# Five of sixteen feed-forward jobs turned in 32x32 blocks on VectorE and through DRAM, with layer norms and low parts moved in the order

## The chip, the cores and the metric

The kernel runs on one core of one Trainium2 chip. The time is the device time of one execution in microseconds (us). Engines are named as in the profile: PE is TensorE's matmuls and PEld its weight loads, DVE is VectorE, ACT is ScalarE, POOL is GpSimd, and SP is the queue from which most transfers are issued.

## The reference, cut to what matters

x is 8 batches of 512 tokens by 128 features, float32. Three layers follow one another; each adds to x.

```
x = x + 0.5 * spikes(relu(LN(x) @ W_fc.T)**2 @ W_proj.T)     # feed-forward, "first"
x = x + attention(LN(x))                                     # per batch, see below
x = x + 0.5 * spikes(relu(LN(x) @ W_fc.T)**2 @ W_proj.T)     # feed-forward, "second"

attention(h): h = LN(h)*gamma + beta; keys = h@Wk.T + bk; values = h@Wv.T + bv
    w = exp((keys@Wka.T + bka)/sqrt(128)); w = w / cumsum(w, tokens)
    return cumsum(w * keys, tokens) * values
```

The spike count of a value is a staircase with five levels, made from two straight lines and a maximum.

## The kernel before, in words

**Jobs.** One feed-forward layer of one batch is a job. There are 16: jobs 0 to 7 are the first layer of batches 0 to 7, jobs 8 to 15 the second. Job j works in lane j mod 2, and a lane has one set of buffers. Attention b is the attention of batch b.

**A job.** Layer norm's statistics are made on DVE (L559 to L572), the inverse deviation and the normalised tokens on POOL (L380, L386). TensorE then turns the four 128x128 tiles of `normed` into the bank `work` (`ff_turn`, L866), because a product needs the features on the partitions. ACT rounds the turned input to its high part `in_hi` (L451) and DVE subtracts it for the low part `in_lo` (L632). TensorE expands to four chunks of `hidden`, each as three products of high and low parts (L853, L854, L857); ACT makes the relu (L455) and its square (L460) of each chunk; TensorE contracts the squares into `work`, in four chunks of 8 instructions (L932), of which chunk 3 ends the job's y. ACT makes the two stairs from it (L464, L467), DVE the maximum, the count and the new x.

**The order.** Nothing is scheduled at run time. Every engine has a loop over steps -3 to 18, and its instructions are written out in that order; semaphores alone tie the engines together. In step i TensorE does, in this order: turn job i; contract chunk 2 of job i-1; turn attention b of the step into `att_work` (L963); contract chunk 3 of job i-1; expand chunks 0 and 1 of job i; turn back the attention of step i-2 (L987); the key attention (a product of three); expand chunks 2 and 3; contract chunk 0; the keys (three); contract chunk 1; the values of the attention of step i-1 (three). `ATT_STEP` gives the steps of attentions 0 to 7: 3, 4, 5, 7, 8, 9, 10, 11.

ACT in step i: the square `share_bank` for the attention of step i-1 (L516, waits for `pooled` of the attention before it), the stairs of job i-1, the relus and squares of job i with the attention's weight and guess between them, then `in_hi` of job i+1 and the attention's high part.

DVE in step i: layer norm of job i+1; `weight_key` of the attention of step i-1 (L706); `pooled` of step i-2 (L723); `in_lo` of job i; `attended` (L731); `att_lo` (L637); `near_share` (L713); the new x of job i-2 (L693); statistics of the next attention with `highest` between (L672); adding the attention to x (L736); `share_key` (L718); `count` (L685); the scan `weight_sum` (L699); in steps 0 to 2 also the attention's weights and biases.

POOL in step i: normalises job i+2, then the attention of step i+2, then makes `guess_sum` and `guess_share` of the attention of step i+1 (L408, L416).

**Waits that matter here.** TensorE turns attention b into `att_work` only when `weight_key` of attention b-1 has read that bank (L960). The transfer that brings x is issued on SP for all batches at the start; the results are stored from SP as they come.

Of the kernel before, what the change touches and what calls it, by code (L numbers as in the profile page):

```python
# [24 lines left out]
P = 128  # L25
F32 = mybir.dt.float32
# [12 lines left out]
FF_JOBS = [("first", b) for b in range(8)] + [("second", b) for b in range(8)]  # L39
ATT_STEP = [3, 4, 5, 7, 8, 9, 10, 11]  # L40
CONTRACT_ORDER = (0, 1, 2, 3)

DVE_SQUARES = [(), ()]
NEXT_TO_LAST_DVE_SQUARES = (1,)
# [6 lines left out]
class FeedForward:  # L51


    def __init__(self, i):
        self.layer, self.batch = FF_JOBS[i]
        self.index, self.lane, self.turn = i, i % 2, i // 2
        self.dve_squares = DVE_SQUARES[i in ATT_STEP] if i < len(FF_JOBS) - 2 else NEXT_TO_LAST_DVE_SQUARES
        self.pool_squares = [c for c in POOL_SQUARES[i in ATT_STEP] if c not in self.dve_squares]
        self.act_squares = [c for c in CONTRACT_ORDER if c not in self.dve_squares and c not in self.pool_squares]
        self.is_last = i == len(FF_JOBS) - 1  # L60
        if self.is_last:
            self.pool_squares, self.dve_squares, self.act_squares = (LAST_SQUARES[e] for e in ("pool", "dve", "act"))

# [4 lines left out]

def feed_forward(i):
    return [FeedForward(i)] if 0 <= i < len(FF_JOBS) else []  # L70


def attention(i):
# [87 lines left out]
def macaron_kernel(nc, x, wk, bk, wka, bka, wv, bv, gamma, beta, w_fc, w_proj, out):  # L161
# [26 lines left out]
    with ExitStack() as ctx:  # L188
        def sb(name, shape, dtype=F32):
            return ctx.enter_context(nc.sbuf_tensor(name, shape, dtype))  # L190
# [50 lines left out]
        rstd = {k: sb(f"rstd_{k}", [P, NT]) for k in KINDS}  # L241
        normed = {k: sb(f"normed_{k}", [P, NT, P]) for k in KINDS}

        in_hi = [sb(f"in_hi{l}", [P, S], F32R) for l in LANES]
        in_lo = [sb(f"in_lo{l}", [P, S], F32R) for l in LANES]
        relu = [sb(f"relu{l}", [P, NC, S]) for l in LANES]
# [41 lines left out]
        ln_args_made, rstd_made = sems("ln_args_made", KINDS), sems("rstd_made", KINDS)  # L288
        normed_made = sems("normed_made", KINDS)
        turned, hi_made, lo_made = sems("turned", KINDS), sems("hi_made", KINDS), sems("lo_made", KINDS)  # L290
        hidden_made, relu_made = sems("hidden_made", LANES), sems("relu_made", LANES)
        squares_act, squares_pool = sems("squares_act", LANES), sems("squares_pool", LANES)
        squares_dve = sems("squares_dve", LANES)
# [17 lines left out]
        def wait_relu(engine, j, c):  # L311

            engine.wait_ge(relu_made[j.lane], NC * j.turn + c + 1)

        def bank_of_hidden(j, c):
            return hidden[(NC * j.index + c) % HIDDEN_BANKS]
# [23 lines left out]
        @block.sync  # L340
        def _(sp):
            load_first_half(sp, 0)
            load_fc_half(sp, 0)
            load_proj_half(sp, 0)
            sp.dma_start(x_of["first"][1][:], x_tiles[1]).then_inc(x_loaded[1], 16)
            for k, w in enumerate((wk, wv, wka)):
                sp.dma_start(att_raw[:, k, :], w).then_inc(att_loaded, 16)
            sp.dma_start(x_of["first"][2][:], x_tiles[2]).then_inc(x_loaded[2], 16)
            for k, v in enumerate((bk, bv, bka, gamma, beta)):
                sp.dma_start(vectors[:, k:k + 1], v.rearrange("(p a) -> p a", a=1)).then_inc(vectors_loaded, 16)  # L350
            for b in range(3, NB):
                sp.dma_start(x_of["first"][b][:], x_tiles[b]).then_inc(x_loaded[b], 16)
            for b in range(NB - 1):
                sp.wait_ge(x_made["out"], b + 1)
                sp.dma_start(out_tiles[b], x_of["out"][b][:]).then_inc(out_stored, 16)
            for t in range(NT):
                sp.wait_ge(x_tile_made, t + 1)
                sp.dma_start(out_tiles[NB - 1][:, t, :], x_of["out"][NB - 1][:, t, :]).then_inc(out_stored, 16)
            sp.wait_ge(out_stored, 16 * (NB - 1 + NT))
# [3 lines left out]
        def _(pool):  # L363
# [14 lines left out]
            def normalise(kind, turn, source):  # L378
# [4 lines left out]
                if turn:  # L383
                    pool.wait_ge(turned[kind], turn)
                for t in range(NT):
                    nc.gpsimd.tensor_scalar(normed[kind][:, t, :], source[:, t, :], neg_mean[kind][:, t:t + 1],  # L386
                                            rstd[kind][:, t:t + 1], ALU.add, ALU.mult).then_inc(normed_made[kind], 1)

            def ff_normalise(j):
                if j.index == 0:  # L390
                    first_inverse_deviation(j)
                else:
                    normalise(j.lane, j.turn, x_of[j.layer][j.batch])

            def att_normalise(b):
                normalise("att", b, x_of["att"][b])

            def ff_squares(j):
                for c in j.pool_squares:
# [17 lines left out]
                                        ALU.mult).then_inc(guess_share_made, 1)  # L417

            for i in range(FIRST_STEP, STEPS):
                for j in feed_forward(i + 2):  # L420
                    ff_normalise(j)
                for b in attention(i + 2):
                    att_normalise(b)
                for b in attention(i + 1):
                    att_guess_sum(b)
                    att_guess_share(b)
                for j in feed_forward(i):
                    ff_squares(j)
# [3 lines left out]
        def _(act):  # L432
# [13 lines left out]
            def ff_hi(j):  # L446
                if j.index == 0:
                    first_hi(j)
                    return
                act.wait_ge(turned[j.lane], j.turn + 1)  # L450
# [105 lines left out]
        def _(dve):  # L556
# [67 lines left out]
            def ff_lo(j):  # L624
                if j.index == 0:
                    dve.wait_ge(hi_made[j.lane], 1)
                    nc.vector.tensor_tensor(in_lo[j.lane][:, HALF:S], first_second_half[:, HALF:S],
                                            in_hi[j.lane][:, HALF:S].bitcast(F32),
                                            ALU.subtract).then_inc(lo_made[j.lane], 1)
                    return  # L630
                dve.wait_ge(hi_made[j.lane], j.turn + 1)
                nc.vector.tensor_tensor(in_lo[j.lane][:], work[j.lane][:], in_hi[j.lane][:].bitcast(F32),  # L632
                                        ALU.subtract).then_inc(lo_made[j.lane], 1)

            def att_part_lo(b):
                dve.wait_ge(hi_made["att"], b + 1)
# [147 lines left out]
            for i in range(FIRST_STEP, STEPS):  # L784
# [3 lines left out]
                for j in feed_forward(i + 1):  # L788
                    if j.index == 0:
                        first_layer_norm(j, 0)  # L790
                        fc_split_ident()
                        first_layer_norm(j, 1)
                        first_normalise(j, 0)
                        first_fc_low_part()
                        first_normalise(j, 1)
                        first_half_lo(j)
                        other_fc_low_parts()
                    else:
                        ff_layer_stats(j)
                for j in feed_forward(i + 1):  # L800
                    if j.index > 0:
                        ff_layer_args(j)
                for b in attention(i - 1):
                    att_weight_key(b)
                for b in attention(i - 2):
                    att_pool(b)
                for j in feed_forward(i):
                    if j.index > 0:
                        ff_lo(j)
                for b in attention(i - 2):  # L810
                    att_product(b)
                for b in attention(i):
# [37 lines left out]
        def _(pe):  # L850
# [6 lines left out]
                return nc.tensor.matmul(dst, w_hi, x_lo, start=False, stop=True)  # L857

            def ff_turn(j):

                if j.turn:
                    pe.wait_ge(stairs_made[j.lane], STAIRS_A_JOB * j.turn)
                for t in range(NT):
                    pe.wait_ge(normed_made[j.lane], NT * j.turn + t + 1)
                    bank_of = first_second_half if j.index == 0 and t >= HALF_TILES else work[j.lane]
                    last = nc.tensor.transpose(bank_of[:, t * P:(t + 1) * P], normed[j.lane][:, t, :], ident[:])  # L866
                    if j.index == 0 and t == HALF_TILES - 1:
                        last.then_inc(first_turned, 1)
                        turn_proj(range(0, NC // 2))
                last.then_inc(turned[j.lane], 1)  # L870
# [203 lines left out]
```

## Time and profile before

| | us |
|---|---|
| median of 3 executions | 147.83 |
| lowest, highest | 147.3, 364.3 |
| the profiled execution | 147.76 |
| its span, first to last instruction | 146.0 |

| engine | busy us | share of the span |
|---|---|---|
| PE | 140.3 | 96% |
| PEld | 126.1 | 86% |
| DVE | 117.3 | 80% |
| ACT | 113.8 | 78% |
| POOL | 95.8 | 66% |

The granted clock of TensorE was 0.999 of full speed over the span. Matmuls overlap one another, so their durations add up to more than the time they take: what one of them costs in a row of matmuls is the distance between two starts. The same holds, more weakly, for DVE and ACT. The DMA engines were busy in the first tenth of the span and with the stores of the end.

### The profile page before, as it was taken

The numbers are of one execution on the slowest core, as the hardware profiler recorded it, in microseconds if no ns is written. First come the engines' busy times: TensorE is split into PE (matmuls) and PEld (weight loads), VectorE is DVE, ScalarE is ACT, GpSimd is POOL, SyncE is SP. The second block draws the span as 40 slices with busy tenths as digits, with TensorE's granted clock in tenths as the row PEclk, the third lists the DMA queues.
The fourth block names the chain that finished last, engine by engine and source line by source line (L and its number), as shares of the span: only waits on it lengthen the run. The fifth ranks groups of instructions, "written<-read, shape, count | busy, mean of one in ns | idle before, by whom it ended". The sixth has DMA issues, their size and how long they took to land.

```text
span 146.0 us, 2901 instructions
## 1 busy us (share of the span) xinstructions
PE 140.3 (96%) x945; PEld 126.1 (86%) x945; DVE 117.3 (80%) x403; ACT 113.8 (78%) x215; POOL 95.8 (66%) x141
## 2 busy tenths in 40 slices
PE   7899999999999999999999999999999999999990
PEld 7689898989989899998988989889789898979790
DVE  3894559388699989999779999999999978453674
ACT  3278877789896996959979697796796977977761
POOL 1439247929999929894998989989967952520300
PEclk9999999999999999999999999999999999999999
DMA  4975000000000000000000000020020102020222
GB/s 140 270 203 161 4 2 0 0 0 4 2 0 2 0 4 2 0 0 0 4 0 0 0 0 7 0 72 0 2 76 0 57 15 72 7 72 0 72 72 72
DMA packets 10510, 5.09 MB, mean 35 GB/s; under 512 B 1152, under 2 KB 10496, under 8 KB 10496
## 3 DMA queue, kind: packets, MB, share of 16 engines
q1 hardware_dynamic: 9808, 4.53, 10.7%
q10 hardware_dynamic: 688, 0.39, 0.9%
q8 instruction: 7, 0.11, 0.3%
q14 instruction: 7, 0.06, 0.1%
HBM read 2.82 MB, written 2.10 MB: 34 GB/s over the span
## 4 chain that ended last, share of the span: by engine, by line
PE 48%; DVE 25%; issue 14%; POOL 6%; DMA 3%; POOLq 1%; ACT 1%; ACTq 1%; DVEq 0%
PE work L932 19%; PE hidden L853 5%; PE hidden L857 5%; PE hidden L854 5%; POOL normed L386 4%; DMA proj_raw<-in_L_ffn_W_proj_dram 3%; DVE weight_sum L699 3%; PE work L866 2%; POOL rstd L380 2%; DVE stats L559 2%; DVE pooled L723 2%; DVE share_bank L713 2%; DVE weight_key L706 2%; DVE share_bank L718 2%; DVE stats_att L559 2%
## 5 line engine op out<-in xcount | busy, mean ns | idle before, releaser
L932 PE MATMUL work<-proj_t,square 128*128 128x128 f32 x480 | 61.2, 275 | 0.0
L932 PEld LDWEIGHTS work<-proj_t,square 128*128 128x128 f32 x480 | 58.8, 192 | 2.4 <-ACT square L460 0.4
L460 ACT ACTIVATE square<-relu 128x512 f32<-128x512 f32 x60 | 37.7, 641 | 0.7
L455 ACT ACTIVATE relu<-hidden 128x512 f32<-128x512 f32 x64 | 36.7, 606 | 0.1
L853 PE MATMUL hidden<-in_hi,fc_lo 128*128 128x512 f32 (+1 forms) x66 | 27.5, 417 | 0.1
L857 PE MATMUL hidden<-in_lo,fc_hi 128*128 128x512 f32 (+1 forms) x66 | 25.6, 387 | 0.0
L854 PE MATMUL hidden<-in_hi,fc_hi 128*128 128x512 f32 (+1 forms) x66 | 25.4, 385 | 0.0
L380 POOL TENSOR_TENSOR rstd<-var_eps,minus_half 128x4 f32<-128x4 f32 x15 | 15.2, 1012 | 14.7 <-DVE neg_mean L572 14.7
L632 DVE TENSOR_TENSOR in_lo<-work,in_hi 128x512 fp32r<-128x512 f32 x15 | 10.2, 680 | 12.3 <-ACT in_hi L451 12.3
L386 POOL TENSOR_SCALAR normed_att<-x_att,neg_mean_att,rstd_att 128x128 f32<-128x128 f32 x32 | 18.1, 578 | 0.8
L386 POOL TENSOR_SCALAR normed<-x_second,neg_mean,rstd 128x128 f32<-128x128 f32 x32 | 16.9, 540 | 0.8
L464 ACT ACTIVATE stairs<-work 128x512 int16<-128x512 f32 (+1 forms) x16 | 9.2, 574 | 7.9 <-PE work L932 6.8
L386 POOL TENSOR_SCALAR normed<-x_first,neg_mean,rstd 128x128 f32<-128x128 f32 x28 | 14.7, 536 | 0.7
L857 PEld LDWEIGHTS hidden<-in_lo,fc_hi 128*128 128x128 f32 x66 | 12.4, 188 | 2.9
L853 PEld LDWEIGHTS hidden<-in_hi,fc_lo 128*128 128x128 f32 x66 | 12.5, 189 | 2.0 <-issue 0.3
L854 PEld LDWEIGHTS hidden<-in_hi,fc_hi 128*128 128x128 f32 x66 | 12.5, 189 | 1.7
L408 POOL TENSOR_TENSOR guess_sum<-weight_sum,guess 128x512 f32<-128x512 f32 x8 | 10.2, 1276 | 5.1 <-ACT guess L509 5.0
L380 POOL TENSOR_TENSOR rstd_att<-var_eps_att,minus_half 128x4 f32<-128x4 f32 x8 | 8.1, 1007 | 8.0 <-DVE neg_mean_att L572 8.0
L451 ACT ACTIVATE in_hi<-work 128x512 fp32r<-128x512 f32 x15 | 8.9, 592 | 4.9 <-PE work L866 4.9
L416 POOL TENSOR_TENSOR guess_share<-weight_key,guess 128x512 f32<-128x512 f32 x8 | 10.2, 1272 | 0.1
L699 DVE TENSOR_TENSOR_SCAN weight_sum<-ones,weight 128x512 f32<-128x512 f32 x8 | 9.7, 1217 | 0.4 <-ACT weight L499 0.4
L723 DVE TENSOR_TENSOR_SCAN pooled<-ones,share_bank 128x512 f32<-128x512 f32 x8 | 9.7, 1210 | 0.0
(118 smaller groups left out, 245.8 us busy)
## 6 DMA issues: line engine op xcount, KB each, us to landing
x_first<-_attn_hidden_states_dram SPq DMA_DIRECT2D x7, 256.0 KB, 4.0
out_dram<-x_out SPq DMA_DIRECT2D x7, 256.0 KB, 2.2
out_dram<-x_out SPq DMA_DIRECT2D x4, 64.0 KB, 1.5
x_first<-_attn_hidden_states_dram ACTq DMA_DIRECT2D x1, 128.0 KB, 2.7
x_first<-_attn_hidden_states_dram SPq DMA_DIRECT2D x1, 128.0 KB, 2.4
fc_raw<-in_L_ffn_W_fc_dram SPq DMA_DIRECT2D x1, 128.0 KB, 2.8
fc_raw<-in_L_ffn_W_fc_dram ACTq DMA_DIRECT2D x1, 128.0 KB, 3.3
proj_raw<-in_L_ffn_W_proj_dram SPq DMA_DIRECT2D x1, 128.0 KB, 3.1
```

The costliest lines, as they stand in the source:

```text
L380: nc.gpsimd.tensor_tensor(rstd[kind][:], var_eps[kind][:], minus_half[:], ALU.pow).then_inc(rstd_made[kind], 1)
L386: nc.gpsimd.tensor_scalar(normed[kind][:, t, :], source[:, t, :], neg_mean[kind][:, t:t + 1], rstd[kind][:, t:t + 1], ALU.add, ALU.mult).t ...
L408: nc.gpsimd.tensor_tensor(guess_sum[b % 2][:], weight_sum[b % ATT_SETS][:], guess[b % 2][:], ALU.mult).then_inc(guess_sum_made, 1)
L416: nc.gpsimd.tensor_tensor(guess_share[b % 2][:], weight_key[b % 2][:], guess[b % 2][:], ALU.mult).then_inc(guess_share_made, 1)
L455: nc.scalar.activation(relu[j.lane][:, c, :], bank_of_hidden(j, c)[:], ACT.Relu).then_inc(relu_made[j.lane], 1)
L460: nc.scalar.activation(square[j.lane][:, c, :], relu[j.lane][:, c, :], ACT.Square).then_inc(squares_act[j.lane], 1)
L699: nc.vector.tensor_tensor_scan(weight_sum[b % ATT_SETS][:], ones[:], weight[b % ATT_SETS][:], 0.0, ALU.mult, ALU.add).then_inc(sum_made, 1)
L723: nc.vector.tensor_tensor_scan(pooled[:], ones[:], share_bank[:], 0.0, ALU.mult, ALU.subtract).then_inc(pooled_made, 1)
L853: nc.tensor.matmul(dst, w_lo, x_hi, start=True, stop=False)
L854: nc.tensor.matmul(dst, w_hi, x_hi, start=False, stop=False)
L857: return nc.tensor.matmul(dst, w_hi, x_lo, start=False, stop=True)
L932: last = nc.tensor.matmul(work[j.lane][:, tokens], square[j.lane][:, c, tokens], proj_t[:, c, :], start=(c == 0 and t == 0), stop=(c == NC ...
```

## The change

Jobs 3 to 7 (`BLOCK_TURNED`) are not turned by TensorE any more. For each of them DVE transposes the 32x32 blocks of `normed` (`ff_block_turn`); SP stores the result to DRAM and loads it back in four transfers, one for each 32 partitions, with the blocks in their places (rows of 512 bytes); ACT and DVE then make `in_hi` and `in_lo` from that buffer in SBUF, in a permuted order, instead of from the bank `work`.

With it the order on DVE and POOL changes. `LAYER_NORM_STEP` and `LAYER_NORM_PLACE` set the layer norm of jobs 3 to 7 to: job 3 step 1, middle; job 4 step 1, end; job 5 step 2, middle; job 6 step 2, end; job 7 step 5, top (before: steps 2 to 6, at the top). All other jobs keep theirs. The block turns stand at the end of steps 1, 2, 2, 3 and 5, ahead of the scan `weight_sum`. `in_lo` of jobs 3 to 7 moves to the very top of the job's step, ahead of the layer norm, `weight_key` and `pooled`. The place of `in_hi` on ACT, the end of step j-1, stays.

```diff
+LAYER_NORM_STEP = [-1, 0, 1, 1, 1, 2, 2, 5, 7, 8, 9, 10, 11, 12, 13, 14]
+LAYER_NORM_PLACE = ['top', 'top', 'top', 'middle', 'end', 'middle', 'end', 'top', 'top', 'top', 'top', 'top', 'top', 'top', 'top', 'top']
+BLOCK_TURN_STEP = [1, 2, 2, 3, 5]
+BLOCK_TURNED = [3, 4, 5, 6, 7]
+QUARTER = 32
+BLOCK_SETS = 3
...
+        def turned_before(j):
+            return j.before(lambda other: not other.by_blocks)
+        def blocks_before(j):
+            return j.before(lambda other: other.by_blocks)
+        def by_token(tile):
+            return tile[:].rearrange("p (a t j) -> p t a j", a=P // QUARTER, t=NT)
+        def in_quarters(tile):
+            return tile[:].rearrange("p (t a j) -> p t a j", a=P // QUARTER, t=NT)
...
(SP, ahead of the stores of the results)
+            for k, index in enumerate(BLOCK_TURNED):
+                j = FeedForward(index)
+                sp.wait_ge(blocks_made[j.lane], blocks_before(j) + 1)
+                sp.dma_start(block_rows[k].ap(), blocks[k % BLOCK_SETS][:]).then_inc(blocks_stored[k], 16)
+                sp.wait_ge(blocks_stored[k], 16)
+                quarters = block_rows[k].ap().rearrange("(a i) (b n) -> b i a n", i=QUARTER, b=P // QUARTER)
+                if k >= BLOCK_SETS:
+                    last = FeedForward(BLOCK_TURNED[k - BLOCK_SETS])
+                    sp.wait_ge(lo_made[last.lane], last.turn + 1)
+                for q in range(P // QUARTER):
+                    part = block_turned[k % BLOCK_SETS][q * QUARTER:(q + 1) * QUARTER, :]
+                    sp.dma_start(part.rearrange("p (a n) -> p a n", n=P),
+                                 quarters[q]).then_inc(blocks_loaded[k], 16)
...
(POOL)
+            def wait_ff_read(j):
+                for last in feed_forward(j.index - 2):
+                    if last.by_blocks:
+                        pool.wait_ge(blocks_made[j.lane], blocks_before(j))
+                    else:
+                        pool.wait_ge(turned[j.lane], turned_before(j))
...
             for i in range(FIRST_STEP, STEPS):
-                for j in feed_forward(i + 2):
+                for j in layer_norms(i + 1, "top", "middle"):
                     ff_normalise(j)
                 for b in attention(i + 2):
                     att_normalise(b)
+                for j in layer_norms(i + 1, "end"):
+                    ff_normalise(j)
...
(ACT, ff_hi)
+                if j.by_blocks:
+                    k = BLOCK_TURNED.index(j.index)
+                    act.wait_ge(blocks_loaded[k], 16 * (P // QUARTER))
+                    act.wait_ge(hidden_made[j.lane], NC * j.turn)
+                    nc.scalar.activation(in_quarters(in_hi[j.lane]), by_token(block_turned[k % BLOCK_SETS]),
+                                         ACT.Copy).then_inc(hi_made[j.lane], 1)
+                    return
...
(DVE, ff_lo and the turn)
+                if j.by_blocks:
+                    nc.vector.tensor_tensor(in_quarters(in_lo[j.lane]), by_token(block_turned[BLOCK_TURNED.index(j.index) % BLOCK_SETS]),
+                                            in_quarters(in_hi[j.lane]).bitcast(F32),
+                                            ALU.subtract).then_inc(lo_made[j.lane], 1)
+                    return
+            def ff_block_turn(j):
+                if j.by_blocks:
+                    dve.wait_ge(normed_made[j.lane], NT * (j.turn + 1))
+                    k = BLOCK_TURNED.index(j.index)
+                    if k >= BLOCK_SETS:
+                        dve.wait_ge(blocks_stored[k - BLOCK_SETS], 16)
+                    rows = blocks[k % BLOCK_SETS]
+                    nc.vector.transpose(rows[:].rearrange("p (b t j) -> p t b j", b=P // QUARTER, t=NT),
+                                        normed[j.lane][:].rearrange("p t (b i) -> p t b i", i=QUARTER)
+                                        ).then_inc(blocks_made[j.lane], 1)
...
(DVE, the loop)
+                for j in feed_forward(i):
+                    if j.by_blocks:
+                        ff_lo(j)
+                for j in layer_norms(i, "top"):
+                    if j.index > 0:
                         ff_layer_stats(j)
-                for j in feed_forward(i + 1):
-                    if j.index > 0:
                         ff_layer_args(j)
                 for b in attention(i - 1):
                     att_weight_key(b)
                 for b in attention(i - 2):
                     att_pool(b)
                 for j in feed_forward(i):
-                    if j.index > 0:
+                    if j.index > 0 and not j.by_blocks:
                         ff_lo(j)
+                for j in layer_norms(i, "middle"):
+                    ff_layer_stats(j)
+                    ff_layer_args(j)
...
+                for j in layer_norms(i, "end"):
+                    ff_layer_stats(j)
+                    ff_layer_args(j)
+                for j in block_turns(i):
+                    ff_block_turn(j)
                 for b in attention(i):
                     att_sum(b)
...
(PE)
             def ff_turn(j):
+                if j.by_blocks:
+                    return
...
(PE, ff_contract)
+                if j.by_blocks and c == 0:
+                    pe.wait_ge(stairs_made[j.lane], STAIRS_A_JOB * j.turn)
```

## Rows read from the trace of the kernel before

**Rows 1.** The page: busy us (share of the span) xinstructions.
```profile
PE 140.3 (96%) x945; PEld 126.1 (86%) x945; DVE 117.3 (80%) x403; ACT 113.8 (78%) x215; POOL 95.8 (66%) x141
```
**Rows 2.** Timeline of PE, steps 3 to 5: start us, us, engine, line, what, count.
```profile
28.57 0.60 PE L963 MATMUL att_work<-ident,normed_att 128*128 128x128 f32 x4
...
35.82 0.60 PE L866 MATMUL work<-ident,normed 128*128 128x128 f32 x4
36.26 1.06 PE L932 MATMUL work<-proj_t,square 128*128 128x128 f32 x8
37.15 0.60 PE L963 MATMUL att_work<-ident,normed_att 128*128 128x128 f32 x4
...
45.11 0.60 PE L866 MATMUL work<-ident,normed 128*128 128x128 f32 x4
...
46.44 0.60 PE L963 MATMUL att_work<-ident,normed_att 128*128 128x128 f32 x4
```
**Rows 3.** Timeline of PE, step 11: the same columns, and idle time before it.
```profile
102.60 0.66 PE L963 MATMUL att_work<-ident,normed_att 128*128 128x128 f32 x4 [0.29 <-DVE weight_key L706]
```
**Rows 4.** Timeline of ACT, steps 3 to 6.
```profile
35.98 0.62 ACT L460 ACTIVATE square<-relu 128x512 f32<-128x512 f32 x1
36.50 0.58 ACT L451 ACTIVATE in_hi<-work 128x512 fp32r<-128x512 f32 x1
...
44.70 0.62 ACT L460 ACTIVATE square<-relu 128x512 f32<-128x512 f32 x1
...
56.58 0.69 ACT L516 ACTIVATE share_bank<-guess_sum,off_centre 128x512 f32<-128x512 f32 x1 [0.49 <-DVE pooled L723]
57.34 0.60 ACT L464 ACTIVATE stairs<-work 128x512 int16<-128x512 f32 x1
59.26 1.17 ACT L460 ACTIVATE square<-relu 128x512 f32<-128x512 f32 x2
...
62.10 0.63 ACT L460 ACTIVATE square<-relu 128x512 f32<-128x512 f32 x1
```
**Rows 5.** Timeline of DVE, steps 1, 2, 4 and 5.
```profile
14.10 0.69 DVE L632 TENSOR_TENSOR in_lo<-work,in_hi 128x512 fp32r<-128x512 f32 x1 [2.04 <-ACT in_hi L451]
...
22.10 0.71 DVE L693 SCALAR_TENSOR_TENSOR x_att<-count,x_first 128x512 f32<-128x512 uint16 x1
...
24.30 0.15 DVE L572 TENSOR_REDUCE neg_mean_att<-moments_att 128x4 f32<-128x4 f32 x1
...
28.56 0.69 DVE L632 TENSOR_TENSOR in_lo<-work,in_hi 128x512 fp32r<-128x512 f32 x1 [2.39 <-ACT in_hi L451]
...
43.78 0.85 DVE L559 BATCH_NORM_STATS2 stats<-x_first 128x6 f32<-128x128 f32 x4
...
45.16 0.74 DVE L706 SCALAR_TENSOR_TENSOR weight_key<-att_work,kv_bias,weight 128x512 f32<-128x512 f32 x1
45.82 1.21 DVE L723 TENSOR_TENSOR_SCAN pooled<-ones,share_bank 128x512 f32<-128x512 f32 x1
46.95 0.67 DVE L632 TENSOR_TENSOR in_lo<-work,in_hi 128x512 fp32r<-128x512 f32 x1
47.53 0.74 DVE L731 SCALAR_TENSOR_TENSOR attended<-att_value,kv_bias,pooled 128x512 f32<-128x512 f32 x1
```
**Rows 6.** Timeline of POOL: job 2, attention 0, and the square of step 15.
```profile
12.50 1.01 POOL L380 TENSOR_TENSOR rstd<-var_eps,minus_half 128x4 f32<-128x4 f32 x1
13.61 1.73 POOL L386 TENSOR_SCALAR normed<-x_first,neg_mean,rstd 128x128 f32<-128x128 f32 x4
...
137.39 1.11 POOL L401 TENSOR_TENSOR square<-relu 128x512 f32<-128x512 f32 x1 [8.91 <-ACT relu L455]
```
**Rows 7.** Line L644 on DVE: min/median/max ns, first and last start us.
```profile
L644 DVE TENSOR_TENSOR square<-relu x3: 680/693/1220, 130.8 to 139.0; 128x512 f32<-128x512 f32 x3
```
**Rows 8.** DMA issues: what, queue, count, KB each, us to landing.
```profile
x_first<-_attn_hidden_states_dram SPq DMA_DIRECT2D x7, 256.0 KB, 4.0
out_dram<-x_out SPq DMA_DIRECT2D x7, 256.0 KB, 2.2
```

More of the change, by code:

```diff
@@ L60, in __init__ @@
         self.is_last = i == len(FF_JOBS) - 1
+        self.by_blocks = i in BLOCK_TURNED
         if self.is_last:
@@ L70, in feed_forward, with layer_norms, block_turns @@
     return [FeedForward(i)] if 0 <= i < len(FF_JOBS) else []
+def layer_norms(i, *places):
+    return [FeedForward(k) for k in range(len(FF_JOBS))
+            if LAYER_NORM_STEP[k] == i and LAYER_NORM_PLACE[k] in places]
+def block_turns(i):
+    return [FeedForward(k) for k in BLOCK_TURNED if BLOCK_TURN_STEP[BLOCK_TURNED.index(k)] == i]
 def attention(i):
@@ L242, in macaron_kernel @@
         normed = {k: sb(f"normed_{k}", [P, NT, P]) for k in KINDS}
+        blocks = [sb(f"blocks{k}", [P, S]) for k in range(BLOCK_SETS)]
+        block_turned = [sb(f"block_turned{k}", [P, S]) for k in range(BLOCK_SETS)]
+        block_rows = [nc.dram_tensor(f"block_rows{k}", (P, S), F32) for k in range(len(BLOCK_TURNED))]
         in_hi = [sb(f"in_hi{l}", [P, S], F32R) for l in LANES]
@@ L290, in macaron_kernel @@
         turned, hi_made, lo_made = sems("turned", KINDS), sems("hi_made", KINDS), sems("lo_made", KINDS)
+        blocks_made = sems("blocks_made", LANES)
+        blocks_stored = [sem(f"blocks_stored{k}") for k in range(len(BLOCK_TURNED))]
+        blocks_loaded = [sem(f"blocks_loaded{k}") for k in range(len(BLOCK_TURNED))]
         hidden_made, relu_made = sems("hidden_made", LANES), sems("relu_made", LANES)
@@ L376, in first_inverse_deviation, with normalise @@
                                         minus_half[:, HALF_TILES:NT], ALU.pow).then_inc(rstd_made[j.lane], 1)
-            def normalise(kind, turn, source):
+            def normalise(kind, turn, source, wait_read):
                 pool.wait_ge(ln_args_made[kind], 2 * (turn + 1))
@@ L382, in normalise @@
                 pool.wait_ge(rstd_made[kind], turn + 1)
-                if turn:
-                    pool.wait_ge(turned[kind], turn)
+                wait_read()
                 for t in range(NT):
@@ L387, in normalise, with wait_att_read @@
                                             rstd[kind][:, t:t + 1], ALU.add, ALU.mult).then_inc(normed_made[kind], 1)
+            def wait_ff_read(j):
[4 more added lines that the diff above has]
+                        pool.wait_ge(turned[j.lane], turned_before(j))
+            def wait_att_read(b):
+                if b:
+                    pool.wait_ge(turned["att"], b)
             def ff_normalise(j):
@@ L392, in ff_normalise @@
                 else:
-                    normalise(j.lane, j.turn, x_of[j.layer][j.batch])
+                    normalise(j.lane, j.turn, x_of[j.layer][j.batch], lambda: wait_ff_read(j))
             def att_normalise(b):
-                normalise("att", b, x_of["att"][b])
+                normalise("att", b, x_of["att"][b], lambda: wait_att_read(b))
             def ff_squares(j):
@@ L449, in ff_hi @@
                     return
-                act.wait_ge(turned[j.lane], j.turn + 1)
+                if j.by_blocks:
[5 more added lines that the diff above has]
+                    return
+                act.wait_ge(turned[j.lane], turned_before(j) + 1)
                 nc.scalar.activation(in_hi[j.lane][:], work[j.lane][:], ACT.Copy).then_inc(hi_made[j.lane], 1)
@@ L797, in _ @@
                         other_fc_low_parts()
-                    else:
+                for j in feed_forward(i):
[3 more added lines that the diff above has]
+                    if j.index > 0:
                         ff_layer_stats(j)
-                for j in feed_forward(i + 1):
-                    if j.index > 0:
                         ff_layer_args(j)
```

## The prediction

> **What bounds the kernel now.** I read the page's busy shares first, then the timelines of PE, ACT, DVE and POOL side by side, then the DMA issues. PE is busy 96% of the span [rows 1], but a share alone does not say that it never waits. The timeline does: a turn takes 0.44 us of issue and a chunk of contraction 0.89 (35.82, 36.26, 37.15 [rows 2]). Three products of 512 columns take 0.69 (estimate: twelve products, the turn and 32 contractions of a job, with the attention's parts, fill the 9.29 us from 35.82 to 45.11: 0.44 + 4 x 0.89 + 0.44 + 7 x 0.69 = 9.27 [rows 2]). So step 4 has no gap on PE, and up to step 9 I find none. Later the only attention wait of note is for `weight_key`, 0.29 us at 102.60 [rows 3]. PE is the bound; the other engines' order matters exactly where PE asks for their results. Below, T is the start of the attention's turn on PE (28.57, 37.15, 46.44 in steps 3, 4, 5 [rows 2]), P the start of the step.
>
> **What is removed.** Five turns of 0.44: 2.2 us, all on the bound. Nothing else can be won but the small waits of the last steps, under 1 us together (0.29 is the largest I saw [rows 3]).
>
> **What is added, with cover.** Five block turns on DVE. The trace has none; from below the nearest is a 128x512 pass with PSUM input, 0.58 from start to start (46.95 to 47.53 [rows 5]), from above the scan, 45.82 to 46.95, 1.13. I take 0.6, since a turn is one pass as `in_lo` is. The first four end in steps 1 to 3, where DVE had 2.39 us of idle ahead of `in_lo` [rows 5]; they cost nothing, and each could cost its excess over 0.6 if that cover went. The round trip: a store of 256 KB lands after 2.2 us, a load after 4.0 [rows 8], 6.2 together, in four parts now. Job 3 is turned at about 19.6 (working below), loaded by 25.9, and ACT wants it at 28.0 (its `in_hi` of 0.58 had just ended when DVE's `in_lo` started at 28.56 [rows 5]): 2 us to spare. Job 7 is turned 6 us after T of step 5 and wanted 17 after it: 5 us to spare. SP has nothing else queued until the stores of the second layer. `in_hi` reads SBUF: 0.6 as before, bounds 0.5 and 0.7. `in_lo` has two SBUF inputs now; 0.58 to 0.9 (L644, the other such pass, has median 0.69 and once 1.22 [rows 7]). I take 0.58, as its median is that of `in_lo`.
>
> **What is moved, and what then waits.** This decides. `in_lo` of jobs 3 to 7 now stands ahead of `weight_key` on DVE, and waits for `in_hi`, which ACT makes as the last feed-forward work of the step before. DVE used to be ahead there: in step 4 it did the layer norm and `weight_key` and only then came to wait. Queued behind the wait are `weight_key`, `pooled` and `attended`; PE's attention turn waits for the first, ACT's `share_bank` for the second, PE's turn back for the third.
>
> *Step 3, POOL.* DVE was free for `x_att` at 22.10 and had `neg_mean_att` at 24.30 [rows 5]. Job 5's layer norm, 1.38 us (43.78 to 45.16 [rows 5]), now precedes both: 25.8. But POOL has job 5 first. It gets its statistics at 22.1 + 1.38 = 23.5; a normalisation takes 12.50 to 15.34, 2.84 [rows 6]; so attention 0 is ready at 23.5 + 2 x 2.84 = 29.2. PE starts that turn at 28.57 - 0.44 = 28.13 and would have its last tile at 28.5. Loss about 0.6 (bounds 0 and 1.2). Likewise job 3: after `in_lo` of job 1, 14.10 + 0.58 [rows 5], a layer norm of 1.38 and 2.84 on POOL make 18.9, and the turn ends at 19.6.
>
> *Step 4.* `in_hi` starts 0.52 after the last square (35.98, 36.50 [rows 4]), 7.93 after T of step 3, and ACT's chain from there on hangs on PE's contraction, so this distance stays. It ends at T + 8.53. Then `in_lo` 0.58, `weight_key` 0.75 (45.16 [rows 5]), signals 0.06 as at 102.60: PE can turn at T + 9.9. It would like to at 35.82 + 0.89 - 28.57 = 8.1. Loss 1.8.
>
> *Step 5.* The same, with the last square 7.55 after T (44.70 - 37.15 [rows 2, 4]): `in_hi` ends at T + 8.67, `in_lo` 9.27, and now job 7's layer norm, 1.38, also stands ahead of `weight_key`: 10.65 + 0.75 + 0.06 = 11.5. PE would like 45.11 + 0.89 - 37.15 = 8.85. Loss 2.6.
>
> *Step 6* has no attention turn. T of step 5 is zero here. PE reaches the step at 8.40. The block turn delays the scan and with it ACT by 0.15; `in_hi` ends at 8.8, `in_lo` 9.4, `weight_key` 10.1, `pooled` 11.3. `share_bank`, the stairs, the relus and the squares of ACT follow at the distances of rows 4 (56.58, 57.34, 59.26): square 0 starts at 14.1 and ends at 14.7. PE wants to contract at 13.4. Loss 1.3.
>
> *Step 7.* ACT comes from its stairs to `in_hi` in 5.28 (57.34 to 62.10, and 0.52 [rows 4]), so `in_hi` ends 0.8 after P. `in_lo` 0.6, job 8's layer norm 1.38, `pooled` 1.13, `attended` 0.74: P + 4.7, where the turn back wants it at 0.89 + 0.44 + 0.89 + 1.39 = 3.6; the low part behind it adds 0.15. Loss 1.3. In step 8 the scan of step 7 and the next layer norm leave DVE 0.3 late. After that job 8 is turned by PE again, DVE and PE meet at `att_lo`, and the old order holds: nothing more.
>
> **The sum.** 0.6 + 1.8 + 2.6 + 1.3 + 1.3 + 0.3 = 7.9, less 2.2: +5.7 on the profiled execution's 147.76, which is the median of 147.83 for practical purposes (the outlier of 364.3 left out). That is **153.5 us**.
>
> One term of it could be larger. In the trace a DVE pass with two SBUF inputs went to 1.22 us once [rows 7], beside POOL's 1.11 us square [rows 6]; the others took 0.69. `guess_sum` runs on POOL about when the new `in_lo` starts in steps 4 to 6, so up to 0.3 in each is open.
>
> The Trainium skill, "SBUF — State Buffer", section "Who interferes with whom", has it that a VectorE instruction with two SBUF inputs and a GpSimd instruction that reads SBUF exclude one another, the later one waiting for the earlier to end. By that rule `in_lo` is held each time, the loss is about 0.9 in all and the time 154.4; by the median of the row it is not held and stays at 153.5. The 1.22 us of the trace agrees with the rule.
>
> The skill's "VectorE: DVE Perf Modes", section "Rules for kernel authors", would leave a 128x128 transpose to TensorE where PSUM will do. No row of this case shows the two ways side by side.
>
> **Rivals.**
> - *The turns come off and nothing waits.* If `in_hi` were there whenever DVE gets to `in_lo`, `weight_key` would not be late, and the time is 147.76 - 2.2 = 145.6, not slower. For it: DVE was late and never idle from 45.16 on in step 5 [rows 5]. Against it: that was with `in_lo` behind 3.2 us of other work. It decides below a wait for `in_hi` of the slack that `weight_key` had, 46.44 - 45.91 = 0.5 [rows 2, 5]; I find 1.5 to 3. Chance 0.08.
> - *Only the two waits for `weight_key` are real.* POOL is in time in step 3, and `pooled` and `attended` of steps 6 and 7 find slack that I don't see, since those are chains over three engines. 147.76 + 1.8 + 2.6 - 2.2 = 150.0. Chance 0.19.
> - *The round trip is late.* If the four loads went one after another at 2.2 us each behind the store, 11 us instead of 6.2, job 3 would be ready at 30.6 and the path would wait some 2.7 us more: 156.2. Against it: the first loads of the kernel overlapped, and step 7 has room. Chance 0.07.
> - *The forecast*, 153.5, in the bounds of its terms: 151 with half of the small losses, 156 with block turns of 1.1 ahead of the scan of step 5 (+0.5), held low parts (+0.9) and the upper end in step 3 (+0.6). Chance 0.66.
>
> **Range and chances.** 149.0 to 156.5 holds the forecast, most of the rival at 150.0 and part of the third. A measurement of this kernel tells 2% from no change, so 144.9 and 150.8 are the limits. Faster: only if the waits of the last steps went with the turns, 0.03. Within 2%: the first rival, most of the second and the low tail of the forecast, 0.28. Slower: 0.69.
>
> **What would show it.** Right: PE gains a gap of 1.5 to 2 us before the attention's turn of step 4 and of 2 to 3 us before that of step 5, put down to DVE `weight_key`; DVE idles before `in_lo` of jobs 4 to 7, put down to ACT `in_hi`, and in no case to a DMA; the step from 8 on is as long as before. Wrong: steps 3 to 7 on PE each 0.44 shorter without gaps (first rival), ACT's `in_hi` waiting for a load (third), or DVE so far behind that `in_hi` is long ready, when DVE and not the order would be what costs.

## The result and the profile after

The changed kernel takes 157.57 us (median of 4 executions, 157.17 to 157.87) against 147.7: a ratio of 1.064, 95% interval 1.059 to 1.069. It is slower, as forecast, by 9.9 us where 5.7 were forecast; the time lies 1.1 us above the range. The profiled execution has a span of 155.9 us. Comparisons here leave disturbed executions out. A ratio weighs all the executions compared and can differ by up to 0.6% from the quotient of the two medians.

The page of the kernel after, its busy row, its clock row (tenths of full speed in 40 slices) and its transfers through DRAM (KB each, us to landing):

```profile
PE 142.6 (91%) x925; PEld 125.4 (80%) x925; DVE 122.0 (78%) x408; ACT 114.1 (73%) x215; POOL 96.1 (62%) x141
...
PEclk9999999999999969999999999999999999999999
...
block_rows<-blocks SPq DMA_DIRECT2D x5, 256.0 KB, 2.2
block_turned<-block_rows SPq DMA_DIRECT2D x20, 64.0 KB, 1.9
```

PE was 96% busy before [rows 1] and is 91% now, and for one slice its clock is not full. The waits of the kernel after (who, for whom, us in total, times, longest):

```profile
DVE in_lo L703 <- ACT in_hi L517: 8.0, 4, 2.3
PE att_work L1062 <- DVE weight_key L792: 5.4, 3, 3.1
ACT share_bank L586 <- DVE pooled L809: 3.3, 2, 2.8
PE att_value L1086 <- DVE attended L817: 1.2, 2, 0.9
PE att_work L1062 <- POOL normed_att L436: 1.1, 2, 0.6
```

These are the waits that the prediction named, in its order: DVE for `in_hi`, and PE, ACT and PE again for what stands behind it. `in_hi` of the five jobs waits for no load. The timeline of PE shows where they fall:

```profile
28.79 0.33 PE L1062 MATMUL att_work<-ident,normed_att 128*128 128x128 f32 x1 [0.47 <-POOL normed_att L436]
29.71 1.19 PE L1062 MATMUL att_work<-ident,normed_att 128*128 128x128 f32 x3 [0.59 <-POOL normed_att L436]
30.73 1.06 PE L1031 MATMUL work<-proj_t,square 128*128 128x128 f32 x8
...
36.67 1.95 PE L1031 MATMUL work<-proj_t,square 128*128 128x128 f32 x16
40.60 0.66 PE L1062 MATMUL att_work<-ident,normed_att 128*128 128x128 f32 x4 [1.99 <-DVE weight_key L792]
...
48.62 1.05 PE L1031 MATMUL work<-proj_t,square 128*128 128x128 f32 x8
52.80 0.66 PE L1062 MATMUL att_work<-ident,normed_att 128*128 128x128 f32 x4 [3.13 <-DVE weight_key L792]
...
54.25 0.78 PE L949 MATMUL hidden<-in_hi,fc_lo 128*128 128x512 f32 x1
...
57.52 0.48 PE L949 MATMUL att_work<-att_hi,att_w_lo 128*128 128x512 f32 x1
...
62.87 1.95 PE L1031 MATMUL work<-proj_t,square 128*128 128x128 f32 x16
...
69.09 2.02 PE L1031 MATMUL work<-proj_t,square 128*128 128x128 f32 x16
...
71.65 1.05 PE L1031 MATMUL work<-proj_t,square 128*128 128x128 f32 x8
...
76.96 0.50 PE L949 MATMUL att_work<-att_hi,att_w_lo 128*128 128x512 f32 x1
```

With a chunk of contraction at 0.89, a turn at 0.44 and three products at 0.69, each step's loss can be read off (us):

| where | PE would | PE did | lost | forecast |
|---|---|---|---|---|
| step 3, contraction behind the attention's turn | 28.57 | 30.73 | 2.2 | 0.6 |
| step 4, attention's turn | 36.67 + 1.78 = 38.45 | 40.60 | 2.15 | 1.8 |
| step 5, attention's turn | 48.62 + 0.89 = 49.51 | 52.80 | 3.3 | 2.6 |
| step 5, from there to the key attention | 3.16 | 4.72 | 1.6 | none |
| step 6, from its start to chunk 0 | 5.0 | 69.09 - 62.87 = 6.2 | 1.2 | 1.3 |
| step 7, from its start to the key attention | 4.05 | 76.96 - 71.65 = 5.3 | 1.3 | 1.3 |
| step 8 | | | 0.2 | 0.3 |

That is 11.95, less 2.2 for the turns: 9.8 of the 9.9. From step 9 on the steps are as long as before. The fourth row is the clock: mean granted clock of three stretches (stretch, its length, busy us of the engines, PEclk, DMA share, GB/s):

```profile
32.00:53.00 21.00, 15.89 (x101) 13.90 (x100) 15.13 (x48) 14.83 (x28) 12.17 (x18) 1.00 0.18 58
53.00:57.50 4.50, 4.50 (x22) 3.81 (x21) 3.85 (x6) 3.17 (x6) 4.39 (x6) 0.62 0.01 2
```

Behind the wait of 3.13 us the clock is at its lower level, 1.2 GHz, for most of 4.5 us, and a product of 512 columns starts every 0.43 us instead of 0.23.

The timeline of DVE in steps 4 and 5, and of POOL around it:

```profile
38.87 1.01 DVE L703 TENSOR_TENSOR in_lo<-block_turned,in_hi 128x512 fp32r<-128x512 f32 x1 [2.31 <-ACT in_hi L517]
39.81 0.74 DVE L792 SCALAR_TENSOR_TENSOR weight_key<-att_work,kv_bias,weight 128x512 f32<-128x512 f32 x1
...
49.38 1.32 DVE L703 TENSOR_TENSOR in_lo<-block_turned,in_hi 128x512 fp32r<-128x512 f32 x1 [2.00 <-ACT in_hi L517]
50.62 0.86 DVE L629 BATCH_NORM_STATS2 stats<-x_first 128x6 f32<-128x128 f32 x4
...
52.00 0.74 DVE L792 SCALAR_TENSOR_TENSOR weight_key<-att_work,kv_bias,weight 128x512 f32<-128x512 f32 x1
```

```profile
23.68 1.38 POOL L431 TENSOR_TENSOR rstd<-var_eps,minus_half 128x4 f32<-128x4 f32 x1 [0.92 <-DVE neg_mean L642]
25.17 2.04 POOL L436 TENSOR_SCALAR normed<-x_first,neg_mean,rstd 128x128 f32<-128x128 f32 x4
27.18 1.00 POOL L431 TENSOR_TENSOR rstd_att<-var_eps_att,minus_half 128x4 f32<-128x4 f32 x1
28.28 2.22 POOL L436 TENSOR_SCALAR normed_att<-x_att,neg_mean_att,rstd_att 128x128 f32<-128x128 f32 x4
...
48.88 1.26 POOL L469 TENSOR_TENSOR guess_sum<-weight_sum,guess 128x512 f32<-128x512 f32 x1
```

In step 5 `in_lo` takes 1.32 us, and ends 0.56 after POOL's `guess_sum` (48.88 + 1.26 = 50.14, 49.38 + 1.32 = 50.70). I read this as held until POOL was through; a run below tests it. The passes of steps 4 and 6, 1.01 and 0.85 us long, also end 0.55 after `guess_sum`. POOL's normalisations take 3.5 and 3.3 us, where 2.84 was the size beside quiet passes [rows 6]. The kernel before has slower ones too:

```profile
39.74 2.38 POOL L386 TENSOR_SCALAR normed<-x_first,neg_mean,rstd 128x128 f32<-128x128 f32 x4
...
48.95 2.55 POOL L386 TENSOR_SCALAR normed<-x_first,neg_mean,rstd 128x128 f32<-128x128 f32 x4
```

Of its eight groups of four tiles between 21 and 58 us, six took 2.17 to 2.55 us and only two took the 1.73 of [rows 6].

### The profile page after: what moved, and what is told of

It is laid out like the page before. It is cut to its first block, busy times and chain, and to the rows that moved or that the text cites. A ratio compares the mean times of both kernels' runs of the same rounds, so it can differ in the third digit from the quotient of the medians.

```text
span 155.9 us, 2900 instructions
## 1 busy us (share of the span) xinstructions
PE 142.6 (91%) x925; PEld 125.4 (80%) x925; DVE 122.0 (78%) x408; ACT 114.1 (73%) x215; POOL 96.1 (62%) x141
## 4 chain that ended last, share of the span: by engine, by line
DVE 31%; PE 23%; issue 17%; ACT 15%; POOL 11%; POOLq 1%; DVEq 0%; ACTq 0%
PE work L1031 7%; POOL normed L436 6%; ACT square L530 4%; ACT relu L525 4%; DVE pooled L809 3%; DVE stats L629 3%; DVE weight_key L792 3%; DVE weight_sum L785 3%; POOL rstd L431 3%; PE hidden L949 2%; PE hidden L1092 2%; PE hidden L953 2%; PE hidden L950 2%; DVE in_lo L703 2%; DVE att_lo L723 2%
## 5 line engine op out<-in xcount | busy, mean ns | idle before, releaser
L949 PE MATMUL hidden<-in_hi,fc_lo 128*128 128x512 f32 (+1 forms) x66 | 28.2, 428 | 0.4 <-DVE in_lo L690 0.3
L950 PE MATMUL hidden<-in_hi,fc_hi 128*128 128x512 f32 (+1 forms) x66 | 25.9, 392 | 0.0
L436 POOL TENSOR_SCALAR normed_att<-x_att,neg_mean_att,rstd_att 128x128 f32<-128x128 f32 x32 | 18.7, 596 | 0.8
L560 ACT ACTIVATE att_hi<-att_work 128x512 fp32r<-128x512 f32 x8 | 4.8, 597 | 13.4 <-PE att_work L1062 13.4
L436 POOL TENSOR_SCALAR normed<-x_first,neg_mean,rstd 128x128 f32<-128x128 f32 x28 | 13.5, 496 | 1.6 <-PE work L963 0.9
L707 DVE TENSOR_TENSOR in_lo<-work,in_hi 128x512 fp32r<-128x512 f32 x10 | 6.8, 679 | 7.5 <-ACT in_hi L521 7.5
L1062 PE MATMUL att_work<-ident,normed_att 128*128 128x128 f32 x32 | 5.8, 288 | 6.7 <-DVE weight_key L792 5.4
L703 DVE TENSOR_TENSOR in_lo<-block_turned,in_hi 128x512 fp32r<-128x512 f32 x5 | 4.5, 910 | 8.0 <-ACT in_hi L517 8.0
```

The costliest lines, as they stand in the source:

```text
L703: nc.vector.tensor_tensor(in_quarters(in_lo[j.lane]), by_token(block_turned[BLOCK_TURNED.index(j.index) % BLOCK_SETS]), in_quarters(in_hi[ ...
L949: nc.tensor.matmul(dst, w_lo, x_hi, start=True, stop=False)
L950: nc.tensor.matmul(dst, w_hi, x_hi, start=False, stop=False)
```

## The experiments

The kernel before took 147.9 to 148.0 us beside these runs. Behind each time stands its ratio to the kernel before, with the 95% interval. The passages quoted with > are what was expected before the run.

**The low part alone, put back.** In the changed kernel:

```
-                for j in feed_forward(i):
-                    if j.by_blocks:
-                        ff_lo(j)
...
-                    if j.index > 0 and not j.by_blocks:
+                    if j.index > 0:
                         ff_lo(j)
```

> The changed kernel with in_lo of jobs 3 to 7 back behind weight_key and pooled on DVE; all else as changed. Theory (order): DVE no longer waits for in_hi ahead of weight_key, so the losses of 2.15 us in step 4, 3.3 in step 5 (with 1.6 of low granted clock behind it), 1.2 in step 6 and 1.3 in step 7 go; the 2.15 of step 3, where POOL normalises attention 0 late, stays: 157.6 - 9.6 = 148.0 us, range 147 to 149.5. Rival (the block work itself costs: the turns, the round trip, in_lo held by POOL): the losses shrink by half at most, 152 to 155.

150.19 us, 1.011 (1.003 to 1.019). The place of `in_lo` alone is worth 7.4 us of the 9.9. The order theory holds and its rival falls, though 2.2 us more are left than expected. The clock of the stretch from step 3 on, and its PE timeline in step 5:

```profile
30.50:35.00 4.50, 4.43 (x17) 3.81 (x18) 3.40 (x15) 2.53 (x5) 3.43 (x7) 0.62 0.38 118
```

```profile
49.30 0.66 PE L1059 MATMUL att_work<-ident,normed_att 128*128 128x128 f32 x4 [0.27 <-DVE weight_key L792]
...
51.82 0.50 PE L950 MATMUL hidden<-in_lo,fc_hi 128*128 128x512 f32 x1 [0.50 <-DVE in_lo L703]
```

The clock now fell behind the waits for POOL in step 3 (0.47 and 0.60 us), and step 5 has two small waits. Of its four executions the one with a granted clock of 1.0 took 149.62, the one at 0.989 took 150.92.

**The order alone, done to the kernel before.**

```
+                for j in feed_forward(i):
+                    if 3 <= j.index <= 7:
+                        ff_lo(j)
                 for j in feed_forward(i + 1):
...
-                    if j.index > 0:
+                    if j.index > 0 and not 3 <= j.index <= 7:
                         ff_lo(j)
```

> The kernel before with one edit: in_lo of jobs 3 to 7 ahead of the layer norm, weight_key and pooled on DVE. No block turn, no DRAM, TensorE turns all jobs. Theory (order alone): in each of steps 4 to 7 weight_key or pooled and attended wait for in_hi, a low part and a layer norm: about 2.75 us in step 4, 2.65 in step 5, 2.8 in step 6 and 1.2 in step 7, 9.4 in all, 157.2 us, and up to 1.6 more for each wait that brings the granted clock down, so 157 to 162. Rival (the block work costs, the order is hidden): 148 to 150.

160.31 us, 1.080 (1.069 to 1.092). Without a block turn or a byte through DRAM the order costs 12.4 us, more than the whole change. The waits in its PE timeline, steps 4, 5 and 6:

```profile
39.68 0.66 PE L966 MATMUL att_work<-ident,normed_att 128*128 128x128 f32 x4 [2.57 <-DVE weight_key L706]
...
51.76 0.66 PE L966 MATMUL att_work<-ident,normed_att 128*128 128x128 f32 x4 [2.57 <-DVE weight_key L706]
...
67.82 0.66 PE L990 MATMUL att_value<-ident,attended 128*128 128x128 f32 x4 [2.22 <-DVE attended L731]
```

Steps 4 and 5 lose 2.7 us each, step 6 3.0 and step 7 1.5, against 2.75, 2.65, 2.8 and 1.2 worked out. Two waits of the same 2.57 us were followed differently: behind that of step 4 the granted clock stayed at 1.00 (40 to 45 us), behind that of step 5 it was 0.66 (52 to 57 us). The execution at a mean clock of 0.989 took 159.61 us, the one at 0.974 took 161.01.

**Job 7's layer norm behind `weight_key`.**

```
-LAYER_NORM_PLACE = [..., 'end', 'middle', 'end', 'top', 'top', ...]
+LAYER_NORM_PLACE = [..., 'end', 'middle', 'end', 'middle', 'top', ...]
```

> The changed kernel with the layer norm of job 7 in the middle of step 5 instead of at its top, so that it no longer stands ahead of weight_key. Theory: the wait of step 5 shrinks by the 1.38 us of that layer norm, from 3.13 to about 1.75; attended and att_lo behind it then come 0.9 late. If the granted clock fell because the wait was longer than the 1.99 us of step 4, which was followed by no fall, it stays at full speed now and gives 1.6 back: 157.6 - 1.4 - 1.6 + 0.9 = 155.5. Rival: the clock falls after the shorter wait too: 157.1.

156.23 us, 1.055 (1.047 to 1.062). The profiled execution took 157.44, but PE is already 1.0 us late when it reaches step 5 (its contraction starts at 49.65 instead of 48.62), so what follows can be compared. PE's waits in steps 5 and 6:

```profile
52.44 0.66 PE L1062 MATMUL att_work<-ident,normed_att 128*128 128x128 f32 x4 [1.74 <-DVE weight_key L792]
...
66.24 0.66 PE L1086 MATMUL att_value<-ident,attended 128*128 128x128 f32 x4 [1.34 <-DVE attended L817]
```

The wait shrank by 1.39, and the granted clock was 1.0 in all four executions where the changed kernel had 0.988 or 0.989. The 0.7 us short of the expectation is in step 6, which grew by 1.0: `attended` is waited for 1.34 instead of 0.29 there, which I had left out.

**`in_lo` with one input in PSUM.** It subtracts what stands in the bank `work`, so the kernel leaves out the right low parts; the order is the same.

```
                     nc.vector.tensor_tensor(in_quarters(in_lo[j.lane]), by_token(...),
-                                            in_quarters(in_hi[j.lane]).bitcast(F32),
+                                            in_quarters(work[j.lane]),
                                             ALU.subtract).then_inc(lo_made[j.lane], 1)
```

> The changed kernel, but in_lo of jobs 3 to 7 subtracts what stands in the bank work instead of in_hi: it still waits for in_hi and has one input in SBUF and one in PSUM instead of two in SBUF. This changes what is computed and leaves the order as it is. Theory (the pass is held while POOL's guess_sum reads SBUF): in_lo takes 0.69 in steps 4, 5 and 6 instead of 1.01, 1.32 and 0.85, and the waits of PE shrink by the same: 157.6 - 1.1 = 156.5. Rival (the permuted order from SBUF makes it slow): no change, 157.6.

156.10 us, 1.049 (1.040 to 1.058), executions from 154.73 to 156.15, 1.5 faster than the change at the median where 1.1 were expected. The passes of the changed kernel and of this one (min/median/max ns):

```profile
L703 DVE TENSOR_TENSOR in_lo<-block_turned,in_hi x5: 679/848/1317, 28.7 to 72.3; 128x512 fp32r<-128x512 f32 x5
```

```profile
L703 DVE TENSOR_TENSOR in_lo<-block_turned,work x5: 676/689/689, 28.7 to 70.7; 128x512 fp32r<-128x512 f32 x5
...
51.44 1.11 PE L1062 MATMUL att_work<-ident,normed_att 128*128 128x128 f32 x4 [2.51 <-DVE weight_key L792]
...
28.37 1.73 POOL L436 TENSOR_SCALAR normed_att<-x_att,neg_mean_att,rstd_att 128x128 f32<-128x128 f32 x4
```

All five take 0.69 at the most, in the same permuted order from SBUF. So the permutation is free, and it is the pass with a second SBUF input that is held. PE's wait is 0.32 shorter in step 4 and 0.62 in step 5. It works the other way too: attention 0's normalisation, which has `in_lo` of job 3 beside it in both kernels, takes POOL 1.73 us here and 2.22 in the changed kernel, and PE's contraction behind it starts 0.4 us earlier.

**Attention 0 before job 5 on POOL.** In the changed kernel:

```
-LAYER_NORM_PLACE = [..., 'middle', 'end', 'middle', 'end', 'top', ...]
-BLOCK_TURN_STEP = [1, 2, 2, 3, 5]
+LAYER_NORM_PLACE = [..., 'middle', 'end', 'end', 'end', 'top', ...]
+BLOCK_TURN_STEP = [1, 2, 3, 3, 5]
```

> The changed kernel with the layer norm of job 5 at the end of step 2 instead of its middle, so that POOL normalises attention 0 before job 5, and the turn of job 5 in step 3 instead of step 2. in_lo stays ahead of weight_key. Theory (step 3 is lost on POOL's order alone): PE's attention turn of step 3 comes 2.1 us earlier and all behind it: 157.6 - 2.1 = 155.5, with L963's successor no longer waiting for POOL. Rival (what is won in step 3 is lost in step 4, since in_hi of job 4 and DVE were late anyway): 157 to 157.6.

156.97 us, 1.060 (1.052 to 1.067): 0.6 better than the change, where 2.1 were expected. The wait of step 3 went, and that of step 4 grew. The profile is of an execution of 159.47 us at a mean clock of 0.977, so the size of this wait is that execution's own:

```profile
41.62 1.11 PE L1062 MATMUL att_work<-ident,normed_att 128*128 128x128 f32 x4 [3.55 <-DVE weight_key L792]
```

The second of DVE's two turns of step 3 now waits 0.85 us for job 6 on POOL, the scan, the guess and `in_hi` follow later, and `in_lo` took 1.49 us. So the rival was nearer for this kernel, and my theory wrong: most of what is won in step 3 is lost in step 4.

**Both edits.**

> Both: in_lo of jobs 3 to 7 back behind pooled, and attention 0 normalised before job 5 as in the run beside it. Theory: of the losses of the changed kernel only those of step 5 seen with the low part back are left (0.3 waiting for weight_key, 0.5 for in_lo): 147.8 - 2.2 + 0.8 = 146.4, up to 147 if POOL has attention 1 late in step 4, where by its queue it has nothing to spare. Rival (DVE has become the bound, so the turns taken off PE bring nothing): 147.8 or more.

149.32 us, 1.008 (1.004 to 1.012), 0.9 better than the low part alone and 2.9 over what I expected. Its waits on PE:

```profile
36.75 1.22 PE L1059 MATMUL att_work<-ident,normed_att 128*128 128x128 f32 x4 [0.21 <-POOL normed_att L436]
...
47.58 0.66 PE L1059 MATMUL att_work<-ident,normed_att 128*128 128x128 f32 x4 [0.82 <-DVE weight_key L792]
...
50.10 0.50 PE L950 MATMUL hidden<-in_lo,fc_hi 128*128 128x512 f32 x1 [0.51 <-DVE in_lo L703]
```

Step 4 loses 0.4 ahead of the attention's turn and 0.6 in it, waiting tile by tile for POOL, which has normalised attention 0, jobs 5 and 6 and attention 1 in a row; step 5 loses 1.0 and 0.7. With five early layer norms POOL and DVE are late in steps 4 and 5, and that takes the 2.2 us back.

**Job 7's layer norm in step 4, and four jobs.** Both start from the kernel with both edits; the first has `LAYER_NORM_STEP` 4, middle, for job 7, the second `BLOCK_TURNED = [3, 4, 5, 6]` with job 7's layer norm back at the top of step 6.

> As the kernel before it in this list, with the layer norm of job 7 in the middle of step 4, where DVE was seen idle, instead of at the top of step 5. Theory: weight_key of step 5 no longer has it ahead, and PE's waits of 0.3 and 0.5 in step 5 go: 145.7 to 146.0. Rival: attention 1's low part comes later in step 4 and POOL has one normalisation more ahead of attention 2: 146.5 to 147.5.

148.67 us, 1.003 (1.000 to 1.006). The waits of step 5 went, but PE waited 0.8 for `att_lo` in step 4. The profiled execution of this kernel took 149.71 and that of the next 150.09, 1.0 and 1.6 above their medians; PE reaches step 3 0.9 and 1.6 us later in them than with both edits, so the excess arose ahead of the steps compared.

> As low part back and attention first, with only jobs 3 to 6 turned in blocks; job 7 is turned by TensorE and has its layer norm at the top of step 6 as in the kernel before. One turn less is taken off PE (0.44), but steps 5 of DVE and POOL have a layer norm and a turn less. Theory: 147.8 - 1.75 + 0.1 = 146.2. Rival (DVE bound later on): 147 to 148.

148.46 us, 1.005 (1.001 to 1.009). POOL is late in step 4 by the same 0.4 as with five jobs.

**Job 6 later.** Four jobs, job 6's layer norm at the end of step 3, turned in step 4.

> Four jobs in blocks, 3 to 6, with the layer norm of job 6 at the end of step 3 instead of step 2 and its turn in step 4, so that POOL normalises attention 1 before job 6. In the run with four jobs PE lost 0.4 and 0.5 us at the attention turn of step 4 to POOL's late tiles. Theory: those 0.9 come back: 148.46 - 0.9 = 147.5, and PE's wait for normed_att in step 4 is gone. Rival: POOL is then late in step 5 instead: 148.5.

150.93 us, 1.019 (1.015 to 1.024), a miss by 3.4 us. POOL is nearly in time for attention 1, but then has job 6 ahead of `guess_sum` and `guess_share`; DVE waits for these, with the new x and all of the step behind, and PE runs out of hidden banks:

```profile
43.41 0.51 PE L946 MATMUL hidden<-in_hi,fc_lo 128*128 128x512 f32 x1 [2.10 <-ACT relu L525]
```

```profile
42.47 0.70 DVE L799 SCALAR_TENSOR_TENSOR share_bank<-share_bank,guess_share 128x512 f32<-128x512 f32 x1 [3.18 <-POOL guess_share L477]
```

The granted clock is not what it missed by: the two executions at 1.0 took 150.22 and 151.88.

**Three jobs and two.** `in_lo` back; jobs 3 to 5 with job 5's layer norm at the end of step 2, and jobs 3 and 4 alone. The lines are those of the kernel with two jobs; in it job 5's layer norm is at the top again:

```
-LAYER_NORM_STEP = [-1, 0, 1, 1, 1, 2, 2, 5, 7, ...]
-BLOCK_TURN_STEP = [1, 2, 2, 3, 5]
-BLOCK_TURNED = [3, 4, 5, 6, 7]
+LAYER_NORM_STEP = [-1, 0, 1, 1, 1, 4, 5, 6, 7, ...]
+BLOCK_TURN_STEP = [1, 2]
+BLOCK_TURNED = [3, 4]
```

> As two jobs, with job 5 too: its layer norm at the end of step 2, behind attention 0 on POOL, its turn in step 3. Theory: 148.0 - 1.3 + 0.3 (in_lo held in steps 4 and 5) = 147.0. Rival: 148.0.

147.82 us, 0.999 (0.997 to 1.001). In step 5 PE waits 0.64 for `weight_key` and 0.51 for `in_lo`, which took 1.48 us there: what the turns save is paid back.

> in_lo back behind pooled, and only jobs 3 and 4 turned in blocks; jobs 5 to 7 have their layer norm and turn as in the kernel before. Theory (PE is the bound and a turn taken off it is worth 0.44, where nothing else is late): 148.0 - 0.87 + 0.1 for a held in_lo of job 4 = 147.2. Rival (DVE or POOL take back each turn): 148.0 or more.

**147.14 us, 0.995 (0.992 to 0.998)**, the fastest of all, by a margin below 1%. Its page and its `in_lo`:

```profile
PE 139.6 (96%) x937; PEld 125.2 (86%) x937; DVE 118.7 (82%) x405; ACT 113.9 (78%) x215; POOL 95.9 (66%) x141
...
L703 DVE TENSOR_TENSOR in_lo<-block_turned,in_hi x2: 691/764/836, 28.7 to 36.8; 128x512 fp32r<-128x512 f32 x2
```

PE starts the turn of job 8 at 71.27 instead of 71.86, and has no gap above 0.2 us from step 3 on to there. The two turns fall where DVE was idle.

## Why the prediction was right or wrong

**Right: the step that decides.** `in_lo` ahead of `weight_key` waits for `in_hi`, and PE behind it. The single undoing takes away 7.4 of 9.9 us and the single doing costs 12.4, so this is shown, and so is the sign.

**Right: what was costed at nothing.** A block turn takes 0.70 us, 0.63 from start to start (0.6 taken), the store lands after 2.2, the loads after 1.9 each, and `in_hi` from SBUF takes 0.61. No `in_hi` waits for a load. The third rival, the late round trip, falls, and so does the first: the turns did not come off without a wait. The second falls too, since steps 3, 6 and 7 lost 2.2, 1.2 and 1.3.

**Right: steps 6 to 8**, within 0.1 us each. In step 6 the total is right, but not its place: about 0.45 us of it is lost at the turn back, waiting for `attended`, where I had put all of it at chunk 0.

**Wrong: the sum, by 4.1 us, in four terms.**
- *Step 3, POOL*: 0.6 taken, 2.2 measured, above its bound of 1.2. The failing step is "a normalisation takes 12.50 to 15.34, 2.84". They took 3.5 and 3.3, which is 1.1 us of the 1.6. That row was one of the quiet ones: six of eight groups of tiles in the kernel before took 2.17 to 2.55 instead of 1.73, and I did not look beyond it. Why the last one was slow is shown: it ran beside the new `in_lo`, and took 1.73 instead of 2.22 with one input of `in_lo` in PSUM. For the first it is argued only: POOL's 1.38 us `rstd` began inside a DVE pass of `x_att`. And the transposes follow POOL's tiles, so PE waited tile by tile.
- *The clock*: nothing taken, 1.6 measured. I priced a wait at its length alone. The prediction has no term for what TensorE does after it. Shown by the clock rows and by job 7's layer norm moved, which took the fall away in all four executions; how the fall is chosen is open, since the low part put back had it behind the waits of 0.47 and 0.60 us in step 3, and the changed kernel, with the same two waits at the same time, had not.
- *Steps 4 and 5*: 1.8 and 2.6 taken, 2.15 and 3.3 measured. The failing choice is "I take 0.58, as its median is that of `in_lo`". It took 1.01 and 1.32. I had the row with 1.22 [rows 7] and the rule beside it, and went by the median, which was of passes that had POOL to themselves. The rule of the Trainium skill ("SBUF — State Buffer", section "Who interferes with whom"), that a pass with two SBUF inputs and a GpSimd instruction that reads SBUF exclude one another, gave the better number here, and the run with one PSUM input agrees: all five passes at 0.69 or less.

With these, 153.5 + 1.6 + 1.6 + 0.35 + 0.7 = 157.75, less 0.2 for steps 6 and 8: 157.55. That this meets 157.57 so closely is in part luck, as the terms are rounded to 0.1. The range had the held pass and a step 3 of 1.2, but step 3 went 1.0 past that and there was nothing for the clock: without either of the two terms of 1.6 the time would have been 156.0, inside it.

A thing I had not asked: what if `in_lo` had stayed in its place? In the three such orders tried, five turns still did not pay (148.67 to 150.19 us). 2.2 us of PE are bought with layer norms that POOL and DVE must do early, and of the five only the first two were seen to have idle time under them.

## What to carry to other kernels

Moving an instruction up in an in-order queue moves its wait up too: ask what stood ahead of it, whether that used to run during the wait, and who waits for that. Price a pass between VectorE and GpSimd by what the other engine does in that very stretch, and price a wait of TensorE with the clock at its lower level behind it as well as without (1.6 us here), since the length of the wait did not tell which it would be. Work taken off the busiest engine pays only as far as the others have idle time at that place: here for two jobs of five.

## What the hardware showed that I had not expected

TensorE's granted clock fell behind a wait of 3.13 us in step 5 (0.62 over 4.5 us) but not behind one of 1.74 us there. Length alone does not sort the cases: of two waits of 2.57 us in the kernel with only the order changed, one had a fall behind it (0.66 over 5 us) and one had not; and two waits of about 0.5 us in step 3 had one with the low part put back and none in the changed kernel.

A pass of VectorE with two SBUF inputs and a pass of GpSimd cost each other time in both directions. Passes of 0.69 us took up to 1.48 beside a GpSimd pass of 1.26 and ended 0.54 to 0.56 us after it each time, as did the pass of 1.22 in the kernel before [rows 7]; four tiles of GpSimd went from 1.73 to 2.22 beside one such pass.
